# Two half-width products with V, in two consecutive steps, in place of one of 512 columns

## What is computed

```
h = layernorm(x)
q, k, v = clip(h @ Wqkv.T, -8, 8), split in three;  q, k = layernorm(q, k) * w + b, over all 512
scores = q k^T / 4 + slope_h * (key - query), causal
x = x + (softmax(scores) @ v) @ Wout.T
x = x + layernorm(x) @ (sum_k alphas_k * bases_k).T
```

## Time and profile before

| | |
|---|---|
| median of 3 runs | 737.36 us |
| the profiled execution | 744.96 us, span 743.2 us |
| TensorE busy (matmul rows) | 684.0 us, 92% |
| VectorE busy | 575.4 us, 77% |
| ScalarE busy | 411.1 us, 55% |
| GpSimd busy | 312.1 us, 42% |
| mean granted TensorE clock | 0.949 of full speed |
| attention: first product with V to the last | 211.9 to 628.9 us |

### The profile page before, as it was taken

How to read it: one execution, slowest core, us unless ns; L and a number is a source line. 1 busy time by engine, 2 the same in 40 slices (tenths; PEclk the granted TensorE clock), 3 DMA queues, 4 the chain that set the end, 5 groups by cost and what they waited for, 6 DMA issues and landing times.

```text
span 743.2 us, 15974 instructions
## 1 busy us (share of the span) xinstructions
PE 684.0 (92%) x6096; PEld 418.1 (56%) x6096; DVE 575.4 (77%) x990; ACT 411.1 (55%) x855; POOL 312.1 (42%) x403
## 2 busy tenths in 40 slices
PE   3999999987995979999999999999999898499998
PEld 2888888773341535544554554455455442388886
DVE  6799999677993969998997999899899820177664
ACT  4133323232072958877886888788788887222221
POOL 1377777667030622742632633222321333443540
PEclk9999999997586989999999999999999999699999
DMA  8325667788089343434434343343434211444442
GB/s 289 84 69 157 159 171 203 200 216 225 2 238 193 89 121 92 110 98 117 123 94 116 98 121 101 110 119 94 122 99 120 63 26 34 133 132 139 138 140 85
DMA packets 101548, 93.63 MB, mean 126 GB/s; under 512 B 11128, under 2 KB 81400, under 8 KB 101472
## 3 DMA queue, kind: packets, MB, share of 16 engines
q1 hardware_dynamic: 99360, 90.51, 43.4%
q0 software_dynamic: 2112, 2.10, 1.7%
HBM read 57.44 MB, written 33.82 MB: 123 GB/s over the span
## 4 chain that ended last, share of the span: by engine, by line
PE 69%; DVE 12%; issue 8%; DMA 4%; SPq 4%; POOL 2%; ACT 2%; DVEq 0%; POOLq 0%; ACTq 0%
PE ps L1093 22%; PE ps L1128 19%; PE ps L1073 8%; PE ps L1007 5%; PE ps L1009 5%; PE ps L1008 5%; DVE stats L946 2%; PE ps L1015 2%; DVE qk_stat L891 2%; DVE qk L887 2%; PE ps L1069 2%; SPq L429 2%; DMA first_k<-in_bias_rows 1%; DVE x_stat L857 1%; DVE rest L866 1%
## 5 line engine op out<-in xcount | busy, mean ns | idle before, releaser
L946 DVE TENSOR_REDUCE stats<-ps 128x1 f32<-128x512 f32 (+3 forms) x608 | 359.7, 656 | 57.5 <-PE ps L1073 55.6
L776 ACT ACTIVATE probs<-ps 128x512 f32<-128x512 f32 (+2 forms) x640 | 310.0, 560 | 97.6 <-PE ps L1093 97.4
L1073 PE MATMUL ps<-first_k,first_q 54*128 54x128 bf16 (+3 forms) x1152 | 221.5, 285 | 14.4 <-DMA first_k<-in_bias_rows 9.2
L1093 PE MATMUL ps<-second_q,second_k 64*128 64x128 bf16 (+4 forms) x1152 | 207.9, 277 | 0.0
L1093 PE MATMUL ps<-first_q,first_k 54*128 54x512 bf16 (+3 forms) x768 | 198.1, 332 | 10.2 <-issue 10.1
L673 POOL TENSOR_SCALAR_AFFINE_SELECT probs<-probs 128x256 f32<-128x256 f32 x256 | 102.5, 406 | 148.6 <-ACT probs L776 141.5
L1128 PE MATMUL ps<-probs,v_sb 128*32 128x512 f32 (+3 forms) x1536 | 159.1, 502 | 1.8 <-issue 0.8
L1093 PEld LDWEIGHTS ps<-first_q,first_k 54*128 54x128 bf16 x768 | 58.2, 95 | 123.6 <-ACT probs L776 107.2
L1073 PEld LDWEIGHTS ps<-first_k,first_q 54*128 54x128 bf16 x1152 | 92.9, 96 | 59.2 <-DVE stats L946 35.2
L1093 PEld LDWEIGHTS ps<-second_q,second_k 50*128 50x128 bf16 (+1 forms) x1152 | 93.0, 96 | 22.4 <-issue 3.6
L1007 PE MATMUL ps<-wqkv_hi,xt_hi 128*128 128x512 f32 x192 | 77.6, 404 | 0.0
(11 more groups left out here) (79 smaller groups left out, 823.2 us busy)
## 6 DMA issues: line engine op xcount, KB each, us to landing
parts_dram<-parts SPq DMA_DIRECT2D x16, 768.0 KB, 6.3
v_dram<-v_ext SPq DMA_DIRECT2D x16, 512.0 KB, 3.4
v_sb<-v_dram SPq DMA_DIRECT2D x16, 512.0 KB, 4.4
o_dram<-o_sb SPq DMA_DIRECT2D x32, 256.0 KB
first_q<-parts_dram SPq DMA_DIRECT2D x96, 64.0 KB
first_k<-parts_dram SPq DMA_DIRECT2D x96, 64.0 KB
second_q<-parts_dram SPq DMA_DIRECT2D x96, 64.0 KB
second_k<-parts_dram SPq DMA_DIRECT2D x96, 64.0 KB
```

What stands on the lines that cost most here:

```text
L776: act.activation(weights, scores, ACT.Exp, scale=SCALE).then_inc(exp_done, 1)
L946: dve.tensor_reduce(to, scores, AX.X, ALU.max).then_inc(max_taken, 1)
L1073: last = pe.matmul(ps[:, bank, r * cols:(r + 1) * cols], first_q[n % STACKS][rows, hp, i * P:(i + 1) * P], first_k[n % STACKS][rows, hp, k ...
L1093: return pe.matmul(ps[:, bank, r * cols + first:r * cols + last], stack_k[n % STACKS][rows, heads[r] // PAIR, kb * P:(kb + 1) * P], stack_ ...
```

## The change

`weigh` gets a second argument, the part. A unit of 512 columns is done in two parts of 256 columns: part 0 at the step where the whole stood, part 1 one step later. All other units have one part, at the place they had. The waits for the values and for `o_ready` stand with part 0; `exp_done` and the masks are waited for in both parts; `pv_done` is counted with the last part. Only the first part of the first key block starts the accumulation in the bank.

```diff
-            def weigh(w):
+            def weigh(w, part):
...
-                if u == 0:
+                if u == 0 and part == 0:
                     pe.wait_ge(v_loaded[n % 2], 16 * (n // 2 + 1))
-                if kb == 0 and 2 * n + half >= 1:
+                if kb == 0 and part == 0 and 2 * n + half >= 1:
                     pe.wait_ge(o_ready, 2 * n + half)
...
+                parts = 2 if cols == BANK else 1
+                mine = slice(part * cols // parts, (part + 1) * cols // parts)
                 last_kb = (half + 1) * TPB // 2 - 1
                 for j in range(G):
-                    last = pe.matmul(ps[j * VW:(j + 1) * VW, PV_BANK, to:to + cols],
+                    last = pe.matmul(ps[j * VW:(j + 1) * VW, PV_BANK, to + mine.start:to + mine.stop],
                                      v_sb[n % 2][:, kb, j * VW:(j + 1) * VW],
-                                     probs[w % P_SLOTS][:, j, 0:cols],
-                                     start=(kb == 0), stop=(kb == last_kb))
-                last.then_inc(pv_done, 1)
+                                     probs[w % P_SLOTS][:, j, mine],
+                                     start=(kb == 0 and part == 0), stop=(kb == last_kb))
+                if part == parts - 1:
+                    last.then_inc(pv_done, 1)
...
-                            weigh(e // NE * NU + u - 1)
-                        weigh(e // NE * NU + u)
+                            weigh(e // NE * NU + u - 1, 0)
+                        weigh(e // NE * NU + u, 0)
+                e -= 1
+                if 0 <= e < GROUPS * NE:
+                    u = ENTRIES[e % NE][0]
+                    if e % NE == UNIT_END[u] and unit_columns(u)[1] == BANK:
+                        weigh(e // NE * NU + u, 1)
```

## The result

The changed kernel took 755.22 us (median of 4 runs, 752.26 to 756.60), the kernel before 737.14 in the same comparison. The ratio is 1.0228, with a 95% interval of 1.0189 to 1.0266: 18.1 us slower, where the prediction had 25.2 slower. The profiled execution of the changed kernel took 752.26 us, with a span of 750.5.

The account below looks back on a forecast made before the run. TensorE was taken to lead, with VectorE 10% behind. Costs of 23.2 (ways in and out, last group included) and 12.3, less 5.3 and 5 given back, made +25.2 us on 737.4: 762 us, range 744 to 774.

Parts of the forecast that it names:

- The chance that it would be slower: Whole kernel: the changed kernel slower than the kernel before by more than 1%, chance 0.83.
- (a): TensorE, each split block: added filling and draining of the array costs 0.25 us, 22.5 us over 15 groups.
- (b): TensorE, unmasked steps: second half blocks cut pairs of steps sharing the array's halves, 0.82 us a group, 12.3 us.
- (c): Max-pass weight loads: shorter blocks end TensorE's waits for VectorE, giving back 0.35 us a group, 5.3 us.
- (d): Group starts: longer steps 28 to 40 shrink six waits for late shift rows by up to 0.9 us each, 5 us.
- The last group: Group without max pass: half the way-in-and-out cost falls into waits for ScalarE, leaving 0.7 us.
- R2: Rival: half blocks feed VectorE more smoothly, saving TensorE waits of 1.0 us a group; 730 us, chance 0.06.

## Why the prediction was right, and where its sizes were off

The chance that it would be slower, the range (744 to 774) and the mechanism held. The table has the steps around each split, in us a group; "two later" is the difference with the second half two steps later, "bare" is from the two runs with the faster VectorE.

| steps | before | changed | difference | two later | bare | predicted, bare |
|---|---|---|---|---|---|---|
| 9 to 12 (unit 0) | 2.25 | 2.57 | 0.31 | 0.25 | 0.31 | 0.35 |
| 21 to 24 (unit 4) | 2.96 | 3.20 | 0.24 | 0.25 | 0.25 | 0.25 |
| 25 to 28 (unit 5) | 2.88 | 3.27 | 0.39 | 0.07 | 0.42 | 0.46 |
| 29 to 32 (unit 6) | 2.43 | 2.82 | 0.40 | 0.18 | 0.40 | 0.46 |
| 33 to 36 (unit 7) | 2.51 | 2.57 | 0.06 | 0.00 | 0.31 | 0.45 |
| 37 to 39 (unit 8) | 1.94 | 2.14 | 0.20 | 0.15 | 0.34 | 0.35 |
| all others | 9.86 | 9.85 | 0.00 | -0.05 | 0.04 | 0 |
| sum | 24.83 | 26.42 | 1.60 | 0.85 | 2.06 | 2.32 |

(a) The ways in and out: right. In the masked part, where both halves have the same work in each step, a split costs 0.24 to 0.25 us, the number forecast.

(b) The cut pairs: right as a mechanism, shown by the second half block two steps later (0.75 us, of which about 0.1 is the way shared with the transpose). It was mis-sized: bare 2.06 - 6 x 0.25 = 0.56 us a group in place of 0.82, 8.4 us in place of 12.3. The largest error is step 34, taken for a full pair of 0.2 though it has 384 columns and stands beside steps of two heads, where 0.06 was found (0.11 by each step's own first matmul).

(c) Waits for VectorE given back: 0.45 us a group, 6.8 us, where 0.35 and 5.3 were taken. They sit where the prediction put them: of the 0.40 us of unit 6's split everything is paid, of unit 7's only 0.06 of 0.31 (0.16 of 0.36 by each step's own first matmul). The waits of the weight loads themselves shrank less, from 1.0 to 0.7 us in group 5; why the two measures differ is open.

(d) Late shift rows: the term was mis-sized, and its reason was incomplete. The prediction let each of six waits shrink by 0.9 us. In fact all go, 8 us in the medians. The steps 28 to 40 grow by 0.6 us only (7.20 to 7.81); from the first issue of the shift rows to the next group's first score matmul it is 6.4 us (367.19 to 373.62) where 5.6 are usual in the kernel before (369.64 to 375.20). That is the 0.9 of the prediction, but a late group needed up to 7.5 (394.46 to 401.99), so it doesn't end a wait of 1.9 by itself. The rest is that the values now go out 4.4 to 6.3 us ahead of the shift rows, where in the late groups it was 3.6 to 4.4. The likely reason, which no run isolates, is that a longer group gives SP's list of loads more time. Sending the shift rows earlier didn't help; taking the values out of the list ahead of them did. The 8.1 us are the whole effect of that edit, so the waits can be a little less.

The last group: 0.7 us predicted. From its first score matmul to that of its last step it went from 21.2 to 23.4 us, 2.2 more. With the second half two steps later it takes 21.1: so the ways in and out cost nothing there in sum, and the 2.2 us come from where the half block stands: the cut pairs. The prediction counted none for this group, and there it was wrong. Without a max pass the two halves of the array have nothing but the scores of two steps to share. In the kernel before, steps 30 and 31 of this group start 0.01 us apart and take 0.45 us together; in the changed one step 30 runs alone, and its 0.44 us come on top.

Sum: (a) 15 x 1.5 = 22.5, (b) +8.4, (c) -6.8, (d) -8.1, the last group +2.2: +18.2 us, against 18.1 measured. The first three groups, which differ from run to run, are taken for equal to the others. The agreement tests the group sums and (d) only: (b) is what was left over, with 0.25 us for every split, so the parting between (a) and (b) rests on the masked steps. Without (d) the terms give 26.3 us, and the two kernels with the values from ScalarE differ by 25.6. (b), (c) and (d) came out 3.9, 1.5 and 3.1 us lower than predicted, the last group 1.5 higher.

R2, the smoother feeding of VectorE, was no rival at this size, but its mechanism is real: with longer blocks TensorE does stand and wait for VectorE. Between 256 and 1,024 columns a block, 512 behind an odd step is the best of those tried. What stays open: why two halves in one step came out 0.3% faster than whole blocks, with its interval just under 1.

## What to carry to other kernels

Where TensorE leads and work that uses its full height comes between work that runs in its halves, each change between them is paid (0.25 us here for a way in and out), and so is a stretch that doesn't fill both halves evenly: count what stands between two full-height blocks before you cut or move one. A finer interleave pays only while it ends waits for another engine that are worth more than the added ways. To compare the block with what the waiting engine's ring holds is not enough: the three banks here hold about 1.7 us of VectorE's work (an estimate, three times 22.09 us by 39 reductions), and a block of 1.48 us already cost 0.45 us a group. And a wait that alternates from group to group can come from a list of transfers that takes more than half of the group (15 of 24.8 us here): look at what is queued ahead of the late one, and not only at when it was issued.

## What the runs showed of the hardware

- 16 matmuls of 256 columns, four column tiles in turn, took 1.00 to 1.01 us in three blocks, and 8 of 512 the same 1.00: no price for each instruction at these sizes.
- Transfers of 4 KB landed 1.7 us after issue at the least and 7.0 us at the most, with the list of loads on the same queue; with the one load of 512 KB issued from another engine, and some 14 us ahead of them, 3.8 us at the most. That was worth 8 us.
- Sending them two steps earlier raised the middle of their landing time from 2.6 to 3.2 us and gained nothing.
